# A mixed chunk of 42 hidden columns, earlier ones, later masks and fewer shift transfers in a fused two-block kernel

## The chip, the cores and the metric

The kernel runs on one core of a Trainium2 chip. A core has five engines with an instruction stream each: TensorE (PE, its weight loads PEld), VectorE (DVE), ScalarE (ACT), GpSimd (POOL) and SyncE (SP), and 16 DMA engines. The metric is the device time of one execution in microseconds.

## The reference, cut to what matters

The input is 8 sequences of 512 tokens with 256 channels, float32. The model is two gated residual steps. Step 0 adds (multi-head retention of the normalised input) times silu(local-attention network of the same). Step 1 adds (latent causal attention with 16 heads) times silu(mixture of 8 experts, the best two for each token). The local-attention network has two layers; the change touches its second half:

```python
x = x + o @ wo                                    # 8 heads of 64, window 128
h = shift_token(x)                                # second 128 channels: row of the token before
h = (h - mean) / sqrt(var + 1e-05) * lg + lb
a, g = split(h @ w1 + b1, 2)                      # w1: 256 x 1364, so 682 columns each
x = x + (a * gelu(g, approximate=False)) @ w2 + b2
```

## The kernel before, in words

Each engine's program is written out by hand in the order in which it is to run, and semaphores join them; nothing is scheduled by a planner. A sequence is an item: 512 tokens as 4 tiles (NT) of 128. The two layers of the local network make 16 items, numbered through. Stage k (0 to 15) ends item k (output projection, shift, normalisation, up and down projection) and beside it prepares item k+1 (QKV, rotary, heads' norms, scores). Stages 0 to 7 do layer 0 and the retention of the same item ("ret"). Stages 8 to 15 do layer 1 and latent attention and routing ("lat", "behind": the part for the item before; this part is absent in stage 8). Stage 15 ("last") prepares nothing. Then come 71 tiles of 128 routed tokens through the experts, and a final sum.

PSUM is two rings of four banks. Ring A (pA) is emptied by ScalarE, ring D (pD) by VectorE; `ring_a_jobs` and `ring_d_jobs` list the jobs in the order of TensorE's program, and a job waits until the job four banks earlier is emptied.

The parts that the change touches:

- Up projection, `up_projection` (through `project`, L722) in six chunks c of 120 hidden columns, 82 in the last. For each chunk TensorE makes the gate product into ring A and the value product into ring D, each as four instructions over 512 tokens. ScalarE's `gelu` (L1281) reads the gate and waits for the product of chunk c-2, whose buffer it takes. VectorE's `gate_up` (L1717) multiplies value and gelu into `hT`. Ahead of chunk 5 it sets rows from 64 on to one (L1714), and one of them carries the bias b2 through `down_projection`, which takes all six chunks.
- Between the chunks, TensorE does work of the prepared item (turns of heads, L761) and of latent attention (`latent_values` L888, `ranks` L915). VectorE does, behind chunk 0, the sums of squares of tile 3 (L1661), the scalings of tiles 2 and 3 (`scale_qk`, L1665) and the router's choice; behind these come chunks 1 to 5.
- Shifted rows: SP's program starts each stage with eight transfers inside SBUF, two for each tile: 127 rows moved down by one (L566), and the row of the tile before or zeros (L568, L570). VectorE's `shifted_stats` (L1631) waits for each tile by its own semaphore.
- Chain for the prepared item: VectorE's `rotary_parts` (L1655, L1657) and `square_sums`, GpSimd's `rotary_sum` (L1497) and `head_norms` (the roots, L1501), VectorE's `scale_qk`, TensorE's turns.
- Latent attention: VectorE's `clipped` (L1775) takes the scores of a pair of heads from ring D, ScalarE's exponential (L1307) follows, and GpSimd's `causal` (L1513, L1514, L1516) masks in place. The order of GpSimd in the tile loop of a stage is: masks of pair 4+t for t = 0, 1, 2, then the sum and the roots of tile t; behind the loop the masks of pair 7.
- Zeroed rows behind each expert's tokens: SP issues one fixed transfer (L624) and four whose address is read from the counts (L627), and four more inside `fetch(0)`, behind the first expert's first weights (L643) and ahead of the first fetch of tokens (L650), which waits for all of them and for GpSimd's scattered rows (L1527).

## Time and profile before

| quantity | value |
|---|---|
| median of 3 runs | 2845.77 us (2840.29 to 2845.85) |
| profiled execution | 2849.19 us, its span 2847.4 us |
| mean granted TensorE clock | 0.978 |
| VectorE busy | 1546.2 us (54%) |
| ScalarE busy | 1235.8 us (43%) |
| GpSimd busy | 1051.0 us (37%) |
| chain that ended last | PE 65%, issue 13%, DVE 10%, POOL 6%, ACT 3%, DMA 2% |

Busy time is summed over the span, so it mixes stages with different limits. The chain that ended last is followed back from the last instruction, each step to what released it. "Issue" is time for which the profile shows no wait. In the timelines each row is one instruction, or several alike run together, and the bracket behind it says how long the engine had been idle before it and who released it. SPq and ACTq are DMA issues.

### The profile page before, as it was taken

The page shows a single profiled execution, that of the slowest core. Times are in us where ns is not written, and L with a number is a line of the kernel's source. Part 1 is how long each engine was busy: PE and PEld are TensorE (multiplying, and loading weights), DVE is VectorE, ACT ScalarE, POOL GpSimd, SP SyncE. Part 2 cuts the span into 40 slices and gives each one's busy share as a digit, 9 for nine tenths or more (in the row PEclk, how much of TensorE's full clock was granted, in tenths as well). Part 3 has the DMA queues.
Part 4 walks back from the last instruction along what each step waited for, and adds up shares of the span by engine and source line. Part 5 has one row for each costly group of instructions (what it writes and reads, how often), then busy time and mean ns, then how long its engine had stood idle before and what let it go on. Part 6 is the DMA issues. An engine that isn't in the chain of part 4 may idle for free.

```text
span 2847.4 us, 41985 instructions
## 1 busy us (share of the span) xinstructions
PE 2703.8 (95%) x15582; PEld 1833.3 (64%) x15582; DVE 1546.2 (54%) x3730; ACT 1235.8 (43%) x2287; POOL 1051.0 (37%) x726
## 2 busy tenths in 40 slices
PE   6999999999999999999999999999997799999993
PEld 4575757566575757555555555555564578999993
DVE  6565566575666555677676767576855322100004
ACT  4454444545453444545454545454543234222222
POOL 5434243443434243445454536363623122111110
PEclk9999999999999999999999999999998899999997
DMA  4000000000001001101010101010000666899987
GB/s 143 12 16 26 26 16 30 27 27 16 26 16 57 18 24 52 61 5 53 4 53 5 53 4 45 12 39 19 30 34 23 235 247 250 304 365 365 360 334 243
DMA packets 85907, 261.83 MB, mean 92 GB/s; under 512 B 10668, under 2 KB 49916, under 8 KB 67020
## 3 DMA queue, kind: packets, MB, share of 16 engines
q1 hardware_dynamic: 75004, 237.19, 23.0%
q0 software_dynamic: 6480, 17.77, 1.7%
q10 hardware_dynamic: 4224, 4.19, 0.4%
q8 instruction: 128, 2.10, 0.3%
q14 instruction: 71, 0.58, 0.1%
HBM read 210.81 MB, written 44.11 MB: 90 GB/s over the span
## 4 chain that ended last, share of the span: by engine, by line
PE 65%; issue 13%; DVE 10%; POOL 6%; ACT 3%; DMA 2%; SPq 0%; POOLq 0%; DVEq 0%; ACTq 0%
PE s_pD L722 19%; PE s_pA L722 18%; PE s_pD L878 5%; PE s_pA L772 3%; PE s_pD L794 3%; PE s_pA L781 3%; PE s_pA L1167 2%; PE s_pD L1182 2%; POOL acc_s L1598 2%; DVE s_qk L1676 2%; POOL s_rinv L1501 2%; PE s_pA L761 1%; DMA s_z<-s_cur 1%; PE s_pA L733 1%; PE s_pA L888 1%
## 5 line engine op out<-in xcount | busy, mean ns | idle before, releaser
L1507 POOL TENSOR_TENSOR s_qk<-s_qk,s_rrec 128x1024 f32<-128x1024 f32 (+1 forms) x128 | 220.7, 1725 | 502.7 <-DVE s_rrec L1682 502.5
L722 PE MATMUL s_pA<-s_w_wqkv,s_curT 128*128 128x512 f32 x768 | 354.6, 602 | 5.6 <-ACT s_curT L1212 3.7
L1236 ACT ACTIVATE s_qk<-s_qk,s_mx 128x256 f32<-128x256 f32 (+1 forms) x512 | 239.8, 471 | 95.3 <-DVE s_mx L1676 95.3
L1775 DVE TENSOR_SCALAR s_pairs<-s_pD 128x1024 f32<-128x1024 f32 (+1 forms) x192 | 195.0, 1040 | 151.4 <-PE s_pD L878 150.1
L722 PEld LDWEIGHTS s_pA<-s_w_wqkv,s_curT 128*128 128x128 f32 x768 | 142.6, 191 | 176.7 <-issue 163.2
L1501 POOL TENSOR_TENSOR s_rinv<-s_ssq,s_half 128x16 f32<-128x16 f32 x64 | 230.1, 3596 | 59.5 <-DVE s_ssq L1661 59.5
L1598 POOL DMA_INDIRECT acc_s<-s_w_w,s_sq x71 | 68.5, 964 | 470.7 <-ACT s_w_w L1444 463.5
L2139 DVE COPY s_w_wo<-s_pD 128x256 f32<-128x256 f32 x71 | 29.9, 421 | 338.5 <-PE s_pD L1153 338.5
L1466 POOL TENSOR_TENSOR s_rs<-s_ve,s_half 128x4 f32<-128x4 f32 x40 | 42.0, 1050 | 433.4 <-DVE s_ve L1636 433.3
L878 PE MATMUL s_pD<-s_mixer 32*128 32x512 f32 (+3 forms) x1024 | 180.7, 467 | 11.9 <-DVE s_pairs L1775 9.0
L722 PE MATMUL s_pA<-s_zT,s_w_w 128*120 128x512 f32 (+1 forms) x384 | 183.8, 601 | 4.2 <-ACT s_pairs L1281 3.1
L1676 DVE CUSTOM_DVE_ANT_0 s_qk<-s_pA,s_maskw 128x256 f32<-128x256 f32 (+1 forms) x512 | 167.9, 386 | 25.3 <-PE s_pA L772 24.8
L722 PE MATMUL s_pD<-s_zT,s_w_w 128*120 128x512 f32 (+1 forms) x384 | 180.7, 593 | 0.0
L1497 POOL TENSOR_TENSOR s_qk<-s_qk,s_rot 128x1024 f32<-128x1024 f32 x64 | 151.1, 2361 | 51.8 <-DVE s_qk L1657 51.8
L1307 ACT ACTIVATE s_pairs<-s_pairs 128x2560 f32<-128x2560 f32 x64 | 149.7, 2339 | 44.2 <-DVE s_pairs L1775 44.0
L1218 ACT COPY s_qk<-s_pA 128x1024 f32<-128x1024 f32 x64 | 64.8, 1012 | 231.6 <-PE s_pA L722 231.6
L878 PEld LDWEIGHTS s_pD<-s_mixer 32*128 32x128 f32 x1024 | 89.3, 188 | 100.3 <-issue 50.6
L772 PE MATMUL s_pA<-s_qkT 64*128 64x256 f32 (+1 forms) x1024 | 134.2, 380 | 5.7 <-DVE s_mx L1676 3.8
L781 PE MATMUL s_pA<-s_ident,s_qk 128*128 128x128 f32 x896 | 126.9, 282 | 11.4 <-POOL s_qk L1507 6.5
L1665 DVE SCALAR_TENSOR_TENSOR s_qk<-s_rinv,s_qk 128x1024 f32<-128x1024 f32 x64 | 110.9, 1733 | 42.0 <-POOL s_rinv L1501 42.0
L722 PEld LDWEIGHTS s_pD<-s_zT,s_w_w 128*120 128x120 f32 (+1 forms) x384 | 68.6, 179 | 97.1 <-issue 93.1
L1444 ACT ACTIVATE s_w_w<-s_pD,s_w_w 128x256 f32<-128x256 f32 x71 | 33.6, 473 | 219.2 <-PE s_pD L1182 219.2
(268 smaller groups left out, 5724.6 us busy)
## 6 DMA issues: line engine op xcount, KB each, us to landing
s_qkT<-in_m_w SPq DMA_DIRECT2D x48, 1024.0 KB, 6.7
s_v_tm<-in_m_w SPq DMA_DIRECT2D x24, 1024.0 KB, 7.4
s_rot<-in_m_w SPq DMA_DIRECT2D x24, 1024.0 KB, 6.3
s_w_wqkv<-in_m_w SPq DMA_DIRECT2D x23, 1024.0 KB, 7.7
s_qk<-in_m_w SPq DMA_DIRECT2D x23, 1024.0 KB, 5.7
s_w_w<-rows_s SPq DMA_DIRECT2D x71, 129.0 KB, 6.0
s_cur<-in_x SPq DMA_DIRECT2D x8, 512.0 KB, 3.5
xn_s<-s_cur SPq DMA_DIRECT2D x8, 512.0 KB, 2.6
```

Source lines behind the costliest of these rows:

```text
L722: last = nc.tensor.matmul(out, lhs(c), rhs(c), start=(c == 0), stop=(c == n - 1))
L772: last = nc.tensor.matmul(ps[:, place(i) * 256 + lo * P:(place(i) + 1) * 256], qkT[r, h // 2, tile_cols(t)], qkT[r, 4 + h // 2, (t - 1 + l ...
L781: last = nc.tensor.transpose(ps[:, (2 * i + k) * P:(2 * i + k + 1) * P], prob[w % 3][:, i * 256 + k * P:i * 256 + (k + 1) * P], ident[:])
L878: last = nc.tensor.matmul(ps[:, 512 * i + col:512 * i + col + T - kt * P], KT[rows, g % 2, tile_cols(kt)], QT[rows, g % 2, kt * P:T], star ...
L1236: last = nc.scalar.activation(pi, pi, ACT.Exp, scale=-1.0, bias=mx[:, u, i:i + 1], accum_out=rsum[:, u, i:i + 1])
L1307: nc.scalar.activation(ph, ph, ACT.Exp, scale=1.0 / SQ24).then_inc(lexp, 1)
L1497: nc.gpsimd.tensor_tensor(qk[:, t, :], qk[:, t, :], rot[:, t % 2, :], ALU.add)
L1501: nc.gpsimd.tensor_tensor(rinv[:, t, :], ssq[:, t, :], half[:], ALU.pow).then_inc(rinv_rdy, 1)
L1507: nc.gpsimd.tensor_tensor(pi, pi, rrec[:, u, :].unsqueeze(2).broadcast_to((P, 4, 256 - lo)), ALU.mult).then_inc(p_rdy, 1)
L1598: nc.gpsimd.indirect_dma_start(out=S["acc"], out_offset=bass.IndirectOffsetOnAxis(ap=goal[:, w % NX:w % NX + 1], axis=0), in_=m_y[:, w % N ...
L1676: last = nc.vector.tensor_tensor_reduce(out=prob[u % 3][:, h], in0=ps[:, h], in1=maskw[:, lo:256], scale=-1.0, scalar=3e38, op0=ALU.add, o ...
L1775: nc.vector.tensor_scalar(Pl[:, w % SLOTS, :, ROUND_AT[r]:ROUND_AT[r] + ROUND_N[r]], ps[:, :, 0:ROUND_N[r]], 80.0, -80.0, ALU.min, ALU.max ...
```

## The change

- Chunks are now 42, 128, 128, 128, 128, 128 hidden columns. Chunk 0 has one product into ring D: 42 value columns, 22 columns of zeros, 42 gate columns (106 in all, `GATE` = 64). The job ("g", k, 0) leaves ring A. `gelu` of chunk 0 waits for this product and reads its rows 64 to 105; it increments `first_gelu`, for which `gate_up` of chunk 0 waits.
- The ones are set ahead of chunk 0 instead of chunk 5, before the wait for the product, in rows 32 to 63 of its buffer; row 42 carries b2.
- Shifted rows: five transfers instead of eight, two semaphores instead of four. Tiles 0 and 1 move in one transfer of 127 rows by two tiles, with two small ones; tiles 2 and 3 in one, with one small one of two rows.
- Except in the last stage, the masks of the seventh pair (index 6) stand ahead of tile 3's sum, that is behind tile 2's roots and not ahead of tile 2's sum.
- The zeroed rows of experts 4 to 7 are issued by ScalarE in stage 15, behind `values_in`, and not by SP in `fetch(0)`.

```diff
-HCH = 120
+HCH = 128
-HSZ = [min(HCH, HID - HCH * c) for c in range(NHC)]
+HSZ = [HID - HCH * (NHC - 1)] + [HCH] * (NHC - 1)
+HAT = [0] + [HSZ[0] + HCH * c for c in range(NHC - 1)]
+GATE = 64
+ONES = 32
+UPW = GATE + HSZ[0] + 2 * HCH * (NHC - 1)
...
-            if s.here:
+            if s.here and c:
                 j += [("g", k, c)]
...
-                    for t in range(NT):
-                        sp.wait_ge(outD, doneD["wo", k, t // 2])
-                        sp.dma_start(hB[1:P, t, :], cur[k % 2][0:P - 1, t, P:D]).then_inc(shifted[t], 16)
-                        if t == 0:
-                            sp.dma_start(hB[0:1, 0, :], I["zrow"]).then_inc(shifted[t], 16)
+                    for i in range(2):
+                        two = slice(2 * i, 2 * i + 2)
+                        sp.wait_ge(outD, doneD["wo", k, i])
+                        sp.dma_start(hB[1:P, two, :], cur[k % 2][0:P - 1, two, P:D]).then_inc(shifted[i], 16)
+                        if i == 0:
+                            sp.dma_start(hB[0:1, 0, :], I["zrow"]).then_inc(shifted[i], 16)
+                            sp.dma_start(hB[0:1, 1, :], cur[k % 2][P - 1:P, 0, P:D]).then_inc(shifted[i], 16)
                         else:
-                            sp.dma_start(hB[0:1, t, :], cur[k % 2][P - 1:P, t - 1, P:D]).then_inc(shifted[t], 16)
+                            sp.dma_start(hB[0:1, two, :], cur[k % 2][P - 1:P, 1:3, P:D]).then_inc(shifted[i], 16)
...
-            for e in range(E // 2):
-                zero_rows(e)
...
-                    for z in range(E // 2, E):
-                        zero_rows(z)
...
-                n = HSZ[c]
+                n = HCH if c else GATE + HSZ[0]
+                at = GATE + HSZ[0] + 2 * HCH * (c - 1) if c else 0
-                ps = slotA("g", b, c)
-                project(ps[0:n, 0:T], lambda k: W["w1"][:, k, HID + c * HCH:HID + c * HCH + n], lambda k: zT[:, k, :], DC).then_inc(mmA, 1)
+                if c:
+                    ps = slotA("g", b, c)
+                    project(ps, lambda k: W["w1"][:, k, at + HCH:at + 2 * HCH], lambda k: zT[:, k, :], DC).then_inc(mmA, 1)
                 ps = slotD("a", b, c)
-                project(ps[0:n, 0:T], lambda k: W["w1"][:, k, c * HCH:c * HCH + n], lambda k: zT[:, k, :], DC).then_inc(mmD, 1)
+                project(ps[0:n, 0:T], lambda k: W["w1"][:, k, at:at + n], lambda k: zT[:, k, :], DC).then_inc(mmD, 1)
...
-                ps = takeA("g", b, c)
+                at = 0 if c else GATE
+                if c:
+                    ps = takeA("g", b, c)
+                else:
+                    act.wait_ge(mmD, DJ["a", b, 0] + 1)
+                    ps = pD[:, colsD[DJ["a", b, 0]]]
                 if b > 0 or c >= 2:
                     act.wait_ge(outD, doneD["a", b, c - 2] if c >= 2 else doneD["a", b - 1, NHC - 1])
-                nc.scalar.activation(gl_of(b)[c % 2][0:n], ps[0:n, 0:T], ACT.Gelu, bias=W["b1"][0:n, 1, c:c + 1]).then_inc(outA, 1)
+                last = nc.scalar.activation(gl_of(b)[c % 2][0:n], ps[at:at + n, 0:T], ACT.Gelu, bias=W["b1"][at:at + n, 1, c:c + 1])
+                last.then_inc(outA if c else first_gelu, 1)
...
+                    if s.last and u == 5:
+                        act.wait_ge(zero_rdy, 2)
+                        act.wait_ge(weight_rdy, TOPK * LAST + 1)
+                        for e in range(E // 2, E):
+                            n = act.value_load(counts_i[0:1, e:e + 1], min_val=0, max_val=B * T)
+                            act.dma_start(S["rows"][bass.ds(n + e * REG, P), :], zrows).then_inc(zero_in, 16)
...
-                    if s.behind and t < (2 if s.last else 3):
+                    if s.behind and t < 2:
                         causal(b - 1, 4 + t)
+                    if s.behind and not s.last and t == 3:
+                        causal(b - 1, 6)
...
-                if c == NHC - 1:
-                    step(nc.vector.memset(hT_of(b)[NHC - 1][64:HCH], 1.0))
+                if c == 0:
+                    step(nc.vector.memset(hT_of(b)[0][ONES:2 * ONES], 1.0))
                 ps = take("a", b, c)
-                dve.wait_ge(outA, doneA["g", b, c])
+                if c:
+                    dve.wait_ge(outA, doneA["g", b, c])
+                else:
+                    dve.wait_ge(first_gelu, b + 1)
```

## Rows read from the trace of the kernel before

**Rows 1.** The page's first part: busy time and share, by engine.
```profile
PE 2703.8 (95%) x15582; PEld 1833.3 (64%) x15582; DVE 1546.2 (54%) x3730; ACT 1235.8 (43%) x2287; POOL 1051.0 (37%) x726
```

**Rows 2.** Windows: stretch, length, busy (x) PE PEld DVE ACT POOL, clock, DMA, GB/s.
```profile
82.00:1113.60 1031.60, 1023.14 (x5478) 657.34 (x5477) 629.23 (x1558) 482.70 (x1011) 401.44 (x213) 1.00 0.08 27
...
1240.40:2113.00 872.60, 844.78 (x4891) 504.42 (x4890) 615.30 (x1399) 450.74 (x775) 431.77 (x300) 0.99 0.08 27
...
2500.00:2780.00 280.00, 280.00 (x1934) 264.04 (x1933) 24.47 (x114) 64.05 (x116) 37.41 (x39) 1.00 0.95 355
```

**Rows 3.** Timeline, up-projection of stage 3: start, us, instruction, [idle before it, releaser].
```profile
521.20 1.88 PE L722 MATMUL s_pA<-s_zT,s_w_w 128*120 128x512 f32 x4
...
522.43 1.28 ACT L1281 ACT_TABLE_LOAD   x1
...
522.92 1.88 PE L722 MATMUL s_pD<-s_zT,s_w_w 128*120 128x512 f32 x4
...
523.72 0.69 ACT L1281 ACTIVATE s_pairs<-s_pA,s_w_b 120x512 f32<-120x512 f32 x1
...
524.83 0.75 DVE L1717 SCALAR_TENSOR_TENSOR s_pairs<-s_pD,s_w_b,s_pairs 120x512 f32<-120x512 f32 x1 [9.08 <-PE s_pD L722]
```

**Rows 4.** Timeline, end of the chain in stage 10.
```profile
1447.21 1.74 DVE L1665 SCALAR_TENSOR_TENSOR s_qk<-s_rinv,s_qk 128x1024 f32<-128x1024 f32 x1 [2.80 <-POOL s_rinv L1501]
...
1454.42 0.69 ACT L1281 ACTIVATE s_pairs<-s_pA,s_w_b 120x512 f32<-120x512 f32 x1 [5.86 <-DVE s_pairs L1717]
...
1455.16 1.98 PE L722 MATMUL s_pA<-s_zT,s_w_w 128*120 128x512 f32 x4 [0.51 <-ACT s_pairs L1281]
```

**Rows 5.** Groups by line and shape: a full-width weight over 256 columns.
```profile
L722 PE MATMUL s_pD<-s_w_wo,s_sq 128*128 128x256 f32 x512 | 113.2, 379 | 0.0
```

**Rows 6.** Timeline, chunk 5's ones in stage 3.
```profile
544.17 0.48 DVE L1714 MEMSET s_pairs<- 56x512 f32 x1 [0.16 <-issue]
```

**Rows 7.** Timeline, shifted rows and their statistics in stage 10.
```profile
1391.46 0.65 SPq L566 DMA_DIRECT2D s_z<-s_cur  x1
...
1393.81 2.40 SPq L570 DMA_DIRECT2D s_z<-s_cur  x1
...
1406.07 0.29 DVE L1631 BATCH_NORM_STATS2 s_stat<-s_cur 128x6 f32<-128x128 f32 x1 [2.29 <-DMA s_z<-s_cur]
```

**Rows 8.** Windows, while those transfers run.
```profile
1393.00:1398.00 5.00, 5.00 (x46) 2.24 (x46) 1.98 (x3) 0.43 (x1) 0.00 (x0) 1.00 0.07 21
```

**Rows 9.** Timeline, tile 1's scaling and turn in stage 8.
```profile
1149.93 2.64 DVE L1665 SCALAR_TENSOR_TENSOR s_qk<-s_rinv,s_qk 128x1024 f32<-128x1024 f32 x1
...
1153.65 1.04 PE L761 MATMUL s_pA<-s_ident,s_qk 128*128 128x128 f32 x8
```

**Rows 10.** Timeline, VectorE and GpSimd in stage 10.
```profile
1428.15 1.30 DVE L1655 TENSOR_TENSOR s_rot<-s_qk,s_w_fS 128x512 f32<-128x512 f32 x2
...
1431.73 0.73 POOL L1513 TENSOR_TENSOR s_pairs<-s_pairs,s_tri 128x256 f32<-128x256 f32 x1 [0.73 <-ACT s_pairs L1307]
...
1435.32 2.36 POOL L1497 TENSOR_TENSOR s_qk<-s_qk,s_rot 128x1024 f32<-128x1024 f32 x1
...
1435.73 3.12 DVE L1655 TENSOR_TENSOR s_rot<-s_qk,s_w_fS 128x512 f32<-128x512 f32 x2
...
1443.28 3.89 POOL L1501 TENSOR_TENSOR s_rinv<-s_ssq,s_half 128x16 f32<-128x16 f32 x1
```

**Rows 11.** Timeline, stage 15 and the step to the expert tiles.
```profile
2150.33 3.77 PE L722 MATMUL s_pA<-s_zT,s_w_w 128*120 128x512 f32 x4 [1.11 <-ACT s_zT L1254]
...
2223.25 4.29 SPq L627 DMA_DIRECT2D rows_s<-s_w_fC  x4
...
2235.06 0.66 PE L1153 MATMUL s_pD<-s_ident,s_w_w 128*128 128x128 f32 x2 [7.85 <-DMA s_w_w<-rows_s]
```

**Rows 12.** Timeline, scores of stage 8.
```profile
1195.76 2.08 PE L772 MATMUL s_pA<-s_qkT 64*128 64x256 f32 x8 [3.15 <-DVE s_mx L1676]
```

**Rows 13.** Windows, from the same moment.
```profile
1195.10:1201.90 6.80, 6.14 (x30) 4.96 (x32) 2.63 (x16) 5.41 (x15) 5.50 (x4) 0.50 0.00 0
```

More of the change, by code:

```diff
@@ L295, in stream_layers @@
         W = {}
-        by_layer = (("wqkv", [P, DC, 3 * INNER]), ("wo", [P, 4, D]), ("ln", [P, 2, DC]), ("w1", [P, DC, 2 * HID]),
+        by_layer = (("wqkv", [P, DC, 3 * INNER]), ("wo", [P, 4, D]), ("ln", [P, 2, DC]), ("w1", [P, DC, UPW]),
                     ("b1", [HCH, 2, NHC]), ("w2", [HCH, NHC, D]), ("qks", [P, 2, 2, DH]))
@@ L471, in stream_layers @@
         xs_in = sem("xs_in")
-        shifted = [sem(f"shifted{t}") for t in range(NT)]
+        shifted = [sem(f"shifted{i}") for i in range(2)]
         x1_kept = sem("x1_kept")
@@ L495, in stream_layers @@
         shift_rdy = sem("shift_rdy")
+        first_gelu = sem("first_gelu")
         fin_silu = sem("fin_silu")
@@ L624, in _ @@
             sp.dma_start(S["rows"][E * REG:E * REG + P, :], zrows).then_inc(zero_in, 16)
-            def zero_rows(e):
+            for e in range(E // 2):
                 n = sp.value_load(counts_i[0:1, e:e + 1], min_val=0, max_val=B * T)
                 sp.dma_start(S["rows"][bass.ds(n + e * REG, P), :], zrows).then_inc(zero_in, 16)
-            for e in range(E // 2):
-                zero_rows(e)
             sp.wait_ge(table, 1)
@@ L808, in up_projection @@
             def up_projection(b, c):
-                n = HSZ[c]
                 if c == 0:
                     pe.wait_ge(outA, doneA["zT", b, 1])
-                ps = slotA("g", b, c)
-                project(ps[0:n, 0:T], lambda k: W["w1"][:, k, HID + c * HCH:HID + c * HCH + n], lambda k: zT[:, k, :], DC).then_inc(mmA, 1)
+                n = HCH if c else GATE + HSZ[0]
[3 more added lines that the diff above has]
+                    project(ps, lambda k: W["w1"][:, k, at + HCH:at + 2 * HCH], lambda k: zT[:, k, :], DC).then_inc(mmA, 1)
                 ps = slotD("a", b, c)
-                project(ps[0:n, 0:T], lambda k: W["w1"][:, k, c * HCH:c * HCH + n], lambda k: zT[:, k, :], DC).then_inc(mmD, 1)
+                project(ps[0:n, 0:T], lambda k: W["w1"][:, k, at:at + n], lambda k: zT[:, k, :], DC).then_inc(mmD, 1)
             def down_projection(b, i):
-                rows = [min(HCH, HSZ[c] + (c == NHC - 1)) for c in range(NHC)]
+                rows = [HSZ[c] + (c == 0) for c in range(NHC)]
                 if i == 0:
@@ L1700, in shifted_stats @@
                 for t in tiles:
-                    dve.wait_ge(shifted[t], 32 * (b + 1))
+                    dve.wait_ge(shifted[t // 2], (32 if t // 2 else 48) * (b + 1))
                     ln_stats(t, halves(b, t))
@@ L2217, in arrange @@
     r["w_ln"] = np.stack([np.stack([per(g), per(b)], 1) for g, b in zip(a["L0_ffn_ln_g"], a["L0_ffn_ln_b"])], 1)
-    r["w_w1"] = np.stack([ch(w) for w in a["L0_ffn_w1"]], 1)
+    up = []
+    for c in range(NHC):
+        value = a["L0_ffn_w1"][:, :, HAT[c]:HAT[c] + HSZ[c]]
+        gate = a["L0_ffn_w1"][:, :, HID + HAT[c]:HID + HAT[c] + HSZ[c]]
+        room = np.zeros(value.shape[:2] + (0 if c else GATE - HSZ[0],), np.float32)
+        up += [value, room, gate]
+    r["w_w1"] = np.stack([ch(w) for w in np.concatenate(up, 2)], 1)
     b1 = np.zeros((HCH, DEPTH, 2, NHC), np.float32)
@@ L2224, in arrange @@
             for i in range(2):
-                b1[0:n, l, i, c] = a["L0_ffn_b1"][l, i * HID + c * HCH:i * HID + c * HCH + n]
-            w2[0:n, l, c] = a["L0_ffn_w2"][l, c * HCH:c * HCH + n]
-        w2[HSZ[-1], l, NHC - 1] = a["L0_ffn_b2"][l]
+                at = 0 if c or not i else GATE
+                b1[at:at + n, l, i, c] = a["L0_ffn_b1"][l, i * HID + HAT[c]:i * HID + HAT[c] + n]
+            w2[0:n, l, c] = a["L0_ffn_w2"][l, HAT[c]:HAT[c] + n]
+        w2[HSZ[0], l, 0] = a["L0_ffn_b2"][l]
     r["w_b1"], r["w_w2"] = b1, w2
```

## The prediction

> **What bounds the kernel now.** I read the page's first part: TensorE is busy 95% of the span [rows 1]. The table by stretch says where that is a bound [rows 2]: 1023 of 1032 us from 82 to 1113.6 (stages 0 to 7, layer 0 with retention), 280 of 280 in the expert tiles, but 845 of 873 in stages 9 to 14 (layer 1 with latent attention). So I went through one stage of each kind by the timeline. In a retention stage TensorE goes through the up-projection without a gap: one projection starts 1.72 us after the one before (521.20, 522.92), and VectorE has idled 9.08 us before its first product [rows 3]. In a latent stage TensorE arrives at the gate product of chunk 4 and waits 0.51 us for ScalarE's gelu of chunk 3; that gelu had waited 5.86 us for VectorE, which stood behind the router block, which stood behind the scaling of tile 3, which had waited 2.80 us for GpSimd's roots of tile 3 [rows 4]. A latent stage is set by a VectorE/GpSimd chain, and TensorE runs just ahead of it. Saving TensorE work there buys nothing unless the chain shortens too.
>
> **Mixed chunk, stages 0 to 7.** The 682 hidden columns need six chunks before and after, but value and gate of the 42-column chunk now share one product of 106 columns: 11 projections of 12 remain. A projection is four hardware matmuls over 512 columns, 1.72 us by the start times above; the weight's columns (120 before, 128 or 106 after) don't enter the length of the moving side, so I take it unchanged. The down projection keeps six chunks and its count of matmuls; a 128-row weight over 256 columns is in the trace with a mean of 379 ns [rows 5], so zero. Gelu and the VectorE product run along 512 elements whatever the partitions: zero. The first gelu now follows the joint product and reads partitions 64 to 105 of the other PSUM tensor, which no row shows; nearest is the gelu of [rows 3], 0.69 us, bounds 0.6 to 1.4. It stands behind a table load of 1.28 us that starts at 522.43 [rows 3], not behind TensorE (the joint product ends at 522.9), so VectorE's first product stays at 524.8 and costs nothing. TensorE runs 1.72 us further ahead, and no wait of a retention stage is close enough to take that back. 8 stages x 1.72 = **13.8 us**.
>
> **Ones ahead of the wait.** A memset of 0.48 us, with 0.16 before it [rows 6], goes from chunk 5 to chunk 0. In stages 0 to 7 VectorE idles there (the 9.08 us): nothing. In latent stages VectorE has no pause there and the reduction for tile 3's roots stands behind it: 0 to 0.64 us a stage; I come to it below.
>
> **Shifted rows in five transfers.** Before: four transfers of 127 rows of 512 B, each with a small one. SP needs 0.65 us for the first of tile 0 and 2.40 for the small one of tile 1 [rows 7]; eight issues are some 11 us, five some 7. But issue is not what VectorE waits for. While the transfers run the DMA engines are busy 0.07, which is one of 16, at 21 GB/s [rows 8]. At that rate 127 x 512 B take 3.1 us, all four 12.4 us from about 1392.6 (just behind the first issue) to 1405.0, and tile 3's statistics start at 1406.07 after 2.29 us of waiting for them [rows 7]. A pair of tiles is 254 rows. If it too goes to one engine, the last byte lands as before, but tile 2's statistics, which were done in the gap, now come behind it together with tile 3's: the pair ends 0.45 to 0.75 us later; I take 0.45. If it is spread over two or more, it ends up to 3 us earlier. I take one engine, as the row has it. The Trainium skill, DMA: Bandwidth & Descriptors, "Why a DMA increments its semaphore by 16 and not by 1", says that the engine count is the largest one up to 16 that divides the slowest dimension, and gives 127 partitions one engine; by it the pair gets one too. No row shows a pair. In stages 0 to 7 the delay disappears in the 9.08 us.
>
> **Stage 8.** VectorE runs without a pause from the statistics to the scaling of tile 1, which ends at 1152.57 (1149.93 + 2.64); TensorE takes that tile's second turn at 1153.65 now and would be there at 1151.93 [rows 9]. With 0.75 us of delay the tile is ready at 1153.3: **0.3 us** stay of 1.72.
>
> **Stages 9 to 14, the masks of the seventh pair.** Before, GpSimd idled 0.73 us, did the masks (1431.73 to 1435.32), summed tile 2 (2.36), took its roots, summed tile 3 and took its roots, 1443.28 to 1447.17. VectorE and GpSimd don't overlap freely: the two rotary products take 1.30 us alone and 3.12 beside the sum [rows 10]. So I lay the new order out as taking turns. Sum of tile 2 at 1431.0 (the idle time is gone) to 1433.4; VectorE's scaling of tile 1, which stood beside the masks, waits for it to 1434.6; clipping (about 2.3) to 1436.9; roots of tile 2 to 1437.0; then the masks (0.7, 0.7, 1.3 alone) and the rotary work (0.65, 0.65, 1.23) alternate to 1441.9; sum to 1444.25; roots to 1448.15. That is 1.0 us later than 1447.17: the idle time won is less than the collision of masks and rotary that is bought. If the masks ran free beside the rotary work, the roots would come about 1.2 earlier instead. The Trainium skill, SBUF — State Buffer, "Who interferes with whom", has a VectorE operation with two SBUF inputs and a GpSimd operation that reads SBUF exclude each other for a whole instruction; by it the three masks meet the products one by one, as in the sequence above, and the 3.12 agrees. Now the memset makes VectorE's reduction the later input of the roots (0.35), and the transfers add 0.45: **+1.8 us per stage, x6 = +10.8**. Bounds: -1.2 and +3.5 (rival 3). TensorE's 1.72 turn into waiting.
>
> **Stage 15.** No tile is prepared ahead. The first gate product takes four matmuls at the lower clock, 3.77 us [rows 11]; the joint product takes its place, chunk 1 follows 1.8 to 2 us sooner: **1.8 us**.
>
> **Zeroed rows for experts 4 to 7, issued by ScalarE.** Before, SP issued them behind the first expert's weights (2223.25, 4.29 us), and TensorE idled 7.85 us to 2235.06 for the first rows of tokens [rows 11]. After, ScalarE issues them from about 2216.7 on; I take the same 4.29 for it. Queued behind them are the two copies that turn the attention of item 6, now until about 2222.0, against 2221.7 at which VectorE released TensorE: 0.3 us at most, hidden in the 7.85. The fetch then waits for the scattered rows, whose last bytes go out about 2 us before those of the zeros; with the issue time: **2.4 us**, bounds 1 and 5.3. The expert tiles are full on TensorE [rows 2], so this reaches the end.
>
> **The sum.** 13.8 + 0.3 + 1.8 + 2.4 - 10.8 = 7.5 us off the profiled execution's 2849.2 (span 2847.4), so 2841.7. That execution is 3.4 above the median of 2845.8; the same 7.5 off the median: **2838 us**. What a measurement of this kernel can tell from no change is 0.2%, 5.7 us.
>
> **Rivals.**
> 1. The latent chain stays where it is (the turns of masks and rotary fall better, the memset is absorbed): 18.3 us off, 2827.5. For it: the idle 0.73 us is real. Against: the 3.12 us row. 20%.
> 2. The pair of tiles goes to two or more DMA engines: statistics end up to 3 us earlier, and the chain shortens by the 1.2 above; stage 8 keeps its 1.72. 6 x 1.2 + 1.4 more than rival 1 gives: 2819. Against: the 0.07. 12%.
> 3. Slower: TensorE idles about 3 us in one piece before the latent values of group 3 in each latent stage (it comes 1.3 us sooner, and the masks of pair 7, which follow tile 3's roots, end 1.8 later). After 3.15 us of idling at 1195.76 [rows 12] the granted clock was 0.50 for 6.8 us [rows 13], the 1.2 GHz level. A drop behind each of the six costs up to 1.7 us where 3.4 us of matmuls run at it. With a chain of +1.8 that makes +3.5 per stage: 18.3 - 21 = -2.7, so 2848.5. It turns to slower at 3.05 us per stage. For it: the idle piece is as long as that one. Against: the chain, not TensorE, is then the bound, and hides some of it. 18%.
> 4. My forecast: 45%. Others, such as a gelu that is slow from a shifted partition: 5%.
>
> **How the numbers follow.** The forecast's own range is 2833 to 2844, since the chain is worth +1.0 to +2.7 per stage. The range 2819 to 2850 takes in the rivals to their middles. Faster by over 0.2% (below 2840): rivals 1 and 2 and six tenths of mine, 0.61; within 0.2%: the rest of mine and most of rival 3, 0.31; slower 0.08.
>
> **What would show it.** The distance from one stage's first up-projection to the next one's 1.72 us shorter in retention stages. In a latent stage: statistics of tiles 2 and 3 back to back after one wait; roots of tile 3 later against the stage's start; TensorE waiting 2 to 3 us before latent values of group 3; SP issuing five transfers in 7 us. The wait before the first expert tile down from 7.85 to about 5.4. Wrong if latent stages shorten by over 1 us: then the turns or the one-engine reading fail.

## The result

The changed kernel takes 2851.56 us (median of 9 runs, 2850.36 to 2853.39), the kernel before 2845.03 (9 runs, 2840.29 to 2846.19). The ratio is 1.002 with an interval of 1.0012 to 1.0029: slower by 6.5 us, and the interval leaves 1 out. The profiled execution of the change took 2852.14 us (span 2850.4). That of before took 2849.19, some 4 us over its own median, so the two traces differ by only 3.0 us, and the stages below add up to that; the other 3.5 us of the difference of the medians belong to no stage that a trace shows.

I measure a stage from the first matmul of its output projection to that of the next, in the timeline (before, stage 10 begins at 1387.08 and stage 11 at 1530.87: 143.8). "Last" is stage 15 up to the first expert product. The kernels from "eight transfers" on are the experiments. Times in us. The stages are those of one profiled execution, whose own time stands in the column "profiled"; then come the median of the timed runs and the median of the kernel before, run on the same chip. The experiments ran on four chips, between which the kernel before differs by up to 3.8 us, so medians of different rows are compared by their distance from the last column.

| kernel | stages 0 to 7 | stage 8 | 9 to 14 | last | profiled | median | before, same chip |
|---|---|---|---|---|---|---|---|
| before | 1031.6 | 126.8 | 872.5 | 122.1 | 2849.2 | 2845.0 | |
| changed | 1028.9 | 128.4 | 880.4 | 118.1 | 2852.1 | 2851.6 | 2845.0 |
| predicted difference | -13.8 | -0.3 | +10.8 | -4.2 | | -7.5 | |
| measured difference | -2.7 | +1.6 | +7.9 | -4.0 | +3.0 | +6.5 | |
| eight transfers (e1) | 1027.4 | 126.6 | 874.8 | 119.6 | 2845.9 | 2844.2 | 2845.8 |
| 128 rows (e2) | 1019.5 | 127.9 | 888.9 | 118.2 | 2850.3 | 2844.7 | 2845.8 |
| old mask order (e3) | 1028.9 | 128.4 | 882.5 | 120.4 | 2856.1 | 2852.8 | 2845.8 |
| zeros on SP (e4) | 1029.0 | 128.5 | 882.3 | 121.8 | 2858.5 | 2854.5 | 2845.8 |
| spread transfers (e5) | 1029.0 | 126.1 | 862.7 | 117.7 | 2832.2 | 2831.0 | 2845.1 |
| 64 rows (e6) | 1029.0 | 128.4 | 881.1 | 117.5 | 2853.0 | 2853.0 (one run) | 2845.1 |
| eight, old masks (e7) | 1027.4 | 127.0 | 877.1 | 117.2 | 2844.3 | 2844.3 | 2845.1 |
| eight, no memset (e8) | 1027.4 | 127.2 | 870.2 | 117.8 | 2837.8 | 2844.3 | 2845.1 |
| three edits (e9) | 1019.5 | 125.1 | 865.7 | 116.9 | 2823.8 | 2822.1 | 2848.9 |
| three edits, old masks (e10) | 1019.5 | 123.8 | 866.5 | 117.7 | 2824.2 | 2818.6 | 2848.9 |
| before, spread (e11) | 1031.6 | 126.8 | 862.4 | 121.4 | 2839.1 | 2839.1 | 2848.9 |
| filled wait (e12) | 1027.4 | 128.4 | 880.9 | 118.2 | 2851.2 | 2851.5 | 2846.9 |

### The profile page after: what moved, and what is told of

Same layout as the page of the kernel before. It is cut to its first block, busy times and chain, and to the rows that moved or that the text cites. A ratio compares the mean times of both kernels' runs of the same rounds, so it can differ in the third digit from the quotient of the medians.

```text
span 2850.4 us, 41810 instructions
## 1 busy us (share of the span) xinstructions
PE 2702.0 (95%) x15518; PEld 1818.9 (64%) x15518; DVE 1532.7 (54%) x3730; ACT 1237.1 (43%) x2287; POOL 1056.3 (37%) x726
## 4 chain that ended last, share of the span: by engine, by line
PE 63%; issue 14%; DVE 11%; POOL 5%; DMA 4%; ACT 2%; SPq 2%; POOLq 0%; DVEq 0%; ACTq 0%
PE s_pD L724 18%; PE s_pA L724 17%; PE s_pD L882 5%; PE s_pA L774 3%; PE s_pA L783 3%; PE s_pD L796 3%; PE s_pA L1171 2%; PE s_pD L1186 2%; DMA s_z<-s_cur 2%; POOL acc_s L1616 2%; POOL rows_s L1543 1%; PE s_pA L735 1%; PE s_pA L892 1%; PE s_pA L763 1%; DVE s_qk L1694 1%
## 5 line engine op out<-in xcount | busy, mean ns | idle before, releaser
L724 PE MATMUL s_pA<-s_w_wqkv,s_curT 128*128 128x512 f32 x768 | 364.8, 617 | 5.6 <-ACT s_curT L1216 3.7
L724 PE MATMUL s_pD<-s_zT,s_w_w 128*128 128x512 f32 (+1 forms) x384 | 183.0, 599 | 1.1 <-ACT s_zT L1258 1.1
L1513 POOL TENSOR_TENSOR s_qk<-s_qk,s_rot 128x1024 f32<-128x1024 f32 x64 | 151.0, 2359 | 55.1 <-DVE s_qk L1675 55.1
L724 PE MATMUL s_pA<-s_zT,s_w_w 128*128 128x512 f32 x320 | 152.1, 598 | 3.1 <-ACT s_pairs L1290 3.1
L724 PE MATMUL s_pD<-s_w_w,s_pairs 43*128 43x256 f32 x480 | 137.7, 402 | 0.0
L783 PE MATMUL s_pA<-s_ident,s_qk 128*128 128x128 f32 x896 | 126.8, 282 | 3.6 <-POOL s_qk L1523 3.2
```

Source lines behind the costliest of these rows:

```text
L724: last = nc.tensor.matmul(out, lhs(c), rhs(c), start=(c == 0), stop=(c == n - 1))
L783: last = nc.tensor.transpose(ps[:, (2 * i + k) * P:(2 * i + k + 1) * P], prob[w % 3][:, i * 256 + k * P:i * 256 + (k + 1) * P], ident[:])
L1513: nc.gpsimd.tensor_tensor(qk[:, t, :], qk[:, t, :], rot[:, t % 2, :], ALU.add)
```

## The profile after

First the busy times from the page of the profile, answering [rows 1], then the windows that answer to [rows 2] and [rows 8], with one more at 1410.4.

```profile
PE 2702.0 (95%) x15518; PEld 1818.9 (64%) x15518; DVE 1532.7 (54%) x3730; ACT 1237.1 (43%) x2287; POOL 1056.3 (37%) x726
```

```profile
82.30:1111.20 1028.90, 1020.36 (x5446) 651.70 (x5445) 631.23 (x1558) 483.07 (x1011) 401.74 (x213) 1.00 0.08 27
...
1239.70:2120.00 880.30, 845.61 (x4866) 497.02 (x4865) 600.40 (x1398) 451.44 (x775) 436.37 (x300) 0.99 0.08 27
...
1393.00:1398.00 5.00, 5.00 (x45) 2.26 (x45) 1.98 (x3) 0.55 (x1) 0.00 (x0) 1.00 0.07 19
...
1410.40:1413.80 3.40, 3.40 (x5) 1.35 (x4) 3.37 (x4) 0.87 (x1) 2.45 (x3) 0.50 0.00 0
```

TensorE's share is 95% as before; it says nothing. The windows do: in stages 9 to 14 TensorE is still busy for 845.6 us, but in 880 us, not in 873. While the shift transfers run the DMA share is 0.07 as before, at 19 GB/s: a pair of tiles goes to one engine. And at 1410.4, 23.5 us into stage 10, the granted clock is 0.50 for 3.4 us; below, such a stretch is called a drop of the clock. The other five of the stages 9 to 14 have one there too, 24 us in.

The up-projection of stage 3, answering [rows 3]: joint product of 106 columns, table load, gelu of its rows 64 to 105, next product, VectorE.

```profile
519.90 1.88 PE L724 MATMUL s_pD<-s_zT,s_w_w 128*106 128x512 f32 x4
...
521.13 1.28 ACT L1290 ACT_TABLE_LOAD   x1
...
522.43 0.68 ACT L1290 ACTIVATE s_pairs<-s_pD,s_w_b 42x512 f32<-42x512 f32 x1
...
522.49 1.88 PE L724 MATMUL s_pA<-s_zT,s_w_w 128*128 128x512 f32 x4
...
523.25 0.74 DVE L1738 SCALAR_TENSOR_TENSOR s_pairs<-s_pD,s_w_b,s_pairs 42x512 f32<-42x512 f32 x1 [6.75 <-ACT s_pairs L1290]
```

This part went as forecast. The next product starts 2.59 us after the joint one, with a turn of heads between them (before, the value product and that turn stood there); gelu from a shifted partition takes 0.68 us; VectorE waits for ScalarE and TensorE never for either.

The loss in the same stage stands at its end, in the down projection. Groups by shape in a stretch of 129 us around stage 2 (337 to 466), first before, then after:

```profile
L722 PE MATMUL s_pD<-s_w_w,s_pairs 120*128 120x256 f32 x24 | 5.9, 383 | 0.0
...
L722 PE MATMUL s_pD<-s_w_w,s_PT_even 120*128 120x256 f32 x16 | 4.1, 379 | 0.0
...
L722 PE MATMUL s_pD<-s_w_w,s_pairs 83*128 83x256 f32 x8 | 2.4, 379 | 0.0
```

```profile
L724 PE MATMUL s_pD<-s_w_w,s_pairs 128*128 128x256 f32 x24 | 6.9, 396 | 0.0
...
L724 PE MATMUL s_pD<-s_w_w,s_PT_even 128*128 128x256 f32 x16 | 4.1, 379 | 0.0
...
L724 PE MATMUL s_pD<-s_w_w,s_pairs 43*128 43x256 f32 x8 | 2.7, 418 | 0.0
```

The count is 48 in both, but the sum is 12.4 us before and 13.7 after. The eight products over 43 rows take 418 ns and not 379, and of their neighbours over 128 rows some take longer too (mean 396). By their start times, products follow each other in 0.216 us, but in 0.31 to 0.32 us in the two or three steps around each change between 43 and 128 rows, some 12 steps in a stage; with 120 and 83 rows no change has such a step. That is the 1.2 us by which a retention stage missed its 1.72: it went from 129.27 to 128.75, 0.52 less. Why the array does this is not shown.

Stage 10, shifted rows and statistics, answering [rows 7]:

```profile
1391.34 0.72 SPq L572 DMA_DIRECT2D s_z<-s_cur  x1
...
1392.10 4.68 SPq L574 DMA_DIRECT2D s_z<-in_zrow  x1
...
1397.44 0.71 SPq L572 DMA_DIRECT2D s_z<-s_cur  x1
...
1406.60 0.29 DVE L1649 BATCH_NORM_STATS2 s_stat<-s_cur 128x6 f32<-128x128 f32 x1 [4.28 <-DMA s_z<-s_cur]
...
1407.36 0.29 DVE L1649 BATCH_NORM_STATS2 s_stat<-s_cur 128x6 f32<-128x128 f32 x1
...
1408.96 1.14 PE L882 MATMUL s_pD<-s_mixer 32*128 32x384 f32 x8 [2.41 <-DVE s_pairs L1796]
```

Before, only tile 3 was still to do when the wait ended at 1406.07. Now the wait ends at 1406.60 (stage 10 starts 0.12 earlier, so 0.65 late), tile 2 comes first, and tile 3 begins 0.76 behind it: 1.41 us late in all. VectorE's clipping of scores stands behind, TensorE waits 2.41 us for it instead of 1.00, and the clock drops.

Where the 0.65 comes from: the single packets of the trace, 509 before and 511 after, follow each other without a gap of 0.3 us in both kernels, so the rows are never held up by SP's 4.68 us of issuing. They start 0.11 us later against the stage's start and lose some 0.5 more in the first 2 us, before the second pair is issued; from then on the lag stays between 0.6 and 0.8. The same stretch before, then after:

```profile
1392.70:1394.70 2.00, 2.00 (x11) 1.25 (x9) 0.51 (x1) 0.00 (x0) 0.00 (x0) 1.00 0.07 19
```

```profile
1392.70:1394.70 2.00, 2.00 (x11) 1.13 (x9) 0.63 (x1) 0.00 (x0) 0.00 (x0) 1.00 0.06 13
```

Why a pair of tiles starts more slowly than a single tile is not shown.

The same stage's end of chain, answering [rows 10]: rotary products, two of the three masks, the memset, the sum of tile 3, its roots.

```profile
1438.40 1.82 DVE L1673 TENSOR_TENSOR s_rot<-s_qk,s_w_fS 128x512 f32<-128x512 f32 x2
...
1438.65 1.02 POOL L1529 TENSOR_TENSOR s_pairs<-s_pairs,s_tri 128x256 f32<-128x256 f32 x1
...
1440.77 2.24 POOL L1532 TENSOR_TENSOR s_pairs<-s_pairs,s_tri 128x512 f32<-128x512 f32 x1
...
1442.05 0.48 DVE L1732 MEMSET s_pairs<- 32x512 f32 x1 [0.16 <-issue]
...
1442.98 2.35 POOL L1513 TENSOR_TENSOR s_qk<-s_qk,s_rot 128x1024 f32<-128x1024 f32 x1
...
1445.74 3.82 POOL L1517 TENSOR_TENSOR s_rinv<-s_ssq,s_half 128x16 f32<-128x16 f32 x1 [0.41 <-DVE s_ssq L1679]
```

Roots of tile 3 start 58.8 us into the stage, 56.2 before, and they now wait for VectorE's sum of squares (0.41 us), not for GpSimd's own sum.

The step to the expert tiles, answering [rows 11]:

```profile
2221.34 4.19 SPq L634 DMA_DIRECT2D rows_s<-s_w_fC  x4
...
2223.70 3.83 ACTq L1431 DMA_DIRECT2D rows_s<-s_w_fC  x4
...
2238.10 0.66 PE L1157 MATMUL s_pD<-s_ident,s_w_w 128*128 128x128 f32 x2 [3.99 <-DMA s_w_w<-rows_s]
```

TensorE waits 3.99 us instead of 7.85. That is nearly the whole gain of the last stage: TensorE begins this wait 114.1 us into the stage, and 114.2 before.

## The experiments

**e1: the eight transfers back.**

```diff
-sp.dma_start(hB[1:P, two, :], cur[k % 2][0:P - 1, two, P:D]).then_inc(shifted[i], 16)
+sp.dma_start(hB[1:P, t, :], cur[k % 2][0:P - 1, t, P:D]).then_inc(shifted[t], 16)
...
-dve.wait_ge(shifted[t // 2], (32 if t // 2 else 48) * (b + 1))
+dve.wait_ge(shifted[t], 32 * (b + 1))
```

> The changed kernel with the eight shift transfers and four semaphores of before; all else stays. Theory S (the pair transfers make the latent stages late): tile 3's statistics stand 1.3 us earlier in each of the stages 9 to 14, TensorE's wait before the scores of the pair there falls from 2.4 to about 1.0 us, the granted clock no longer drops 24 us into these stages, and a stage goes from 146.5 to about 144 us: about 2 to 2.5 us for each of six, 1 for stage 8, so 2836 to 2840 against 2851.6. Theory C (the chain over masks, memset and roots of tile 3 sets these stages, as predicted): only the transfers' share goes, 0.5 us a stage, so about 2848. Retention stages unchanged at 128.75 by both.

2844.16 us (2839.8 to 2848.53, 10 runs), ratio to before 0.9997 (0.9987 to 1.0007): 7.4 us under the changed kernel (8.1 by the distances from before). In stage 10 (starts at 1381.39), tile 3's statistics, the scores behind them, and tile 3's sum and roots:

```profile
1400.53 0.29 DVE L1647 BATCH_NORM_STATS2 s_stat<-s_cur 128x6 f32<-128x128 f32 x1 [2.37 <-DMA s_z<-s_cur]
...
1402.12 1.14 PE L880 MATMUL s_pD<-s_mixer 32*128 32x384 f32 x8 [1.15 <-DVE s_pairs L1794]
...
1435.65 2.35 POOL L1511 TENSOR_TENSOR s_qk<-s_qk,s_rot 128x1024 f32<-128x1024 f32 x1
...
1438.41 3.82 POOL L1515 TENSOR_TENSOR s_rinv<-s_ssq,s_half 128x16 f32<-128x16 f32 x1 [0.41 <-DVE s_ssq L1677]
```

Tile 3's statistics stand 19.1 us into the stage (19.6 and 20.4 for the two tiles with pairs), TensorE's wait is 1.15 instead of 2.41, and no stage but one has a drop near 24 us. The roots start at 57.0, 1.8 earlier than with pairs, and the stage is 144.6 against 146.4. The signs of theory S came, but not its full size: the time is 2844 and not 2836 to 2840. Stages 9 to 14 are 874.8 and not the 868 or so expected: 0.8 of the 2.6 us at the roots is of other origin (e7, e8), and three stages have drops elsewhere.

**e2: 128 rows of chunk 0 in the down projection.**

```diff
-rows = [HSZ[c] + (c == 0) for c in range(NHC)]
+rows = [HCH] * NHC
...
+nc.vector.memset(hT_of(b)[0][GATE:HCH], 1.0)
```

> The changed kernel with the down projection reading all 128 rows of chunk 0: rows above b2's are set to one and meet weights of zero, so the result is the same; one more memset for each item. Theory W (a product over 43 rows between products over 128 rows costs a gap of 0.1 us at each change, 12 of them in a stage): the gaps go, a retention stage goes from 128.75 to about 127.5, latent stages lose up to 1.2 where TensorE sets them, so 2836 to 2842 against 2851.6. Rival (the gaps come from other work between, such as waits for VectorE's chunk or the order of the chunks): nothing changes but the memset, 2851 to 2853.

2844.70 us (2840.69 to 2851.74, 10 runs), ratio 0.9997. Groups of the same stretch:

```profile
L724 PE MATMUL s_pD<-s_w_w,s_pairs 128*128 128x256 f32 x32 | 8.0, 383 | 0.0
...
L724 PE MATMUL s_pD<-s_w_w,s_PT_even 128*128 128x256 f32 x16 | 4.1, 379 | 0.0
```

12.1 us for the same 48 products. A retention stage is 127.55, so the full 1.72 less than 129.27, and stages 0 to 7 are 9.4 us shorter than with 43 rows. The rival is out. Part of it was lost again: by the medians the edit gains 6.9 us (7.6 by the distances from before). In the profiled execution, which lies 5.6 over the median, stages 9 to 14 grew by 8.5 us. Some 3.7 of these, 0.6 a stage, stand at the roots of tile 3, which now wait 1.04 us for VectorE and not 0.41: the second memset stands ahead of their sum. The rest goes with eight drops of the clock (one of 6.8 us; three of them late, at 119 and 146 us) where there had been six. That the one more memset or the earlier TensorE brings these drops was not told apart.

**e6: 64 rows.**

```diff
-rows = [HSZ[c] + (c == 0) for c in range(NHC)]
+rows = [HCH if c else GATE for c in range(NHC)]
```

> The changed kernel with 64 rows of chunk 0 in the down projection instead of 43; the rows of one above b2's meet weights of zero. Tells what in the 43 rows costs: if it is that they are no more than half of the array's 128 (before, 83 rows cost nothing), a retention stage stays at 128.75 us and the mean of these products near 418 ns; if it is the odd count, it falls to 127.6 us, as with 128 rows.

One run, 2852.98 us. Groups of the same stretch:

```profile
L724 PE MATMUL s_pD<-s_w_w,s_pairs 128*128 128x256 f32 x24 | 6.9, 396 | 0.0
...
L724 PE MATMUL s_pD<-s_w_w,s_PT_even 128*128 128x256 f32 x16 | 4.1, 379 | 0.0
...
L724 PE MATMUL s_pD<-s_w_w,s_pairs 64*128 64x256 f32 x8 | 2.7, 418 | 0.0
```

64 rows cost what 43 do, to the nanosecond, and the stage stays at 128.75. Before, 83 rows cost nothing. So it is the small number of rows beside products over more, not the odd count; where between 64 and 83 rows the cost begins was not measured.

**e3: the masks of the seventh pair back ahead of tile 2's sum.**

```diff
-if s.behind and t < 2:
+if s.behind and t < (2 if s.last else 3):
     causal(b - 1, 4 + t)
-if s.behind and not s.last and t == 3:
-    causal(b - 1, 6)
```

> The changed kernel with the seventh pair's masks back ahead of tile 2's sum. Theory C (as predicted, the masks collide with the rotary products and make tile 3's roots 1.0 us late in stages 9 to 14): 1.0 us a stage back, so about 2845.6. Theory S (the shift transfers and the clock drop at 24 us set these stages): the stages stay within 0.5 us, 2849 to 2854; it may even be slower, as the idle time of GpSimd comes back.

2852.77 us (2850.42 to 2856.82, 6 runs), ratio 1.0026 (1.0013 to 1.0039). Stage 10 starts at 1386.90; sum of tile 3 and its roots:

```profile
1442.90 2.35 POOL L1513 TENSOR_TENSOR s_qk<-s_qk,s_rot 128x1024 f32<-128x1024 f32 x1
...
1445.89 3.82 POOL L1517 TENSOR_TENSOR s_rinv<-s_ssq,s_half 128x16 f32<-128x16 f32 x1 [0.65 <-DVE s_ssq L1677]
```

The roots start at 59.0 with the old order, 58.8 with the new, in all six stages. Theory C is out: the new order does not cost 1.0 us a stage.

**e4: the zeroed rows of experts 4 to 7 back on SP.** The loop with its four issues goes from ScalarE's stage 15 to `fetch(0)`.

> The changed kernel with the zeroed rows of experts 4 to 7 issued by SP behind the first expert's weights, as before. The prediction's step has 2.4 us for them, so 2854; bounds 1 to 5.3. A rival, that the scattered rows and not the zeros end the wait now: under 1 us, 2852. The distance from the last stage's start to the first expert product goes from 118.1 to 120.5 by the first, and stays by the second.

2854.47 us (2853.73 to 2858.5, 5 runs), ratio 1.0035 (1.0021 to 1.0049), 2.9 more than the changed kernel. SP's issues and the first expert product:

```profile
2233.44 4.28 SPq L651 DMA_DIRECT2D rows_s<-s_w_fC  x4
...
2244.02 0.66 PE L1160 MATMUL s_pD<-s_ident,s_w_w 128*128 128x128 f32 x2 [8.33 <-DMA s_w_w<-rows_s]
```

The wait is 8.33 instead of 3.99 us; the distance of "last" is 121.8 against 118.1. The step is worth 2.9 by these medians (2.2 by the distances from before on each chip) and 3.7 by the traces; its rival, under 1 us, is out by the wait.

**e5: 112 and 15 rows instead of 127.**

```diff
-sp.dma_start(hB[1:P, two, :], cur[k % 2][0:P - 1, two, P:D]).then_inc(shifted[i], 16)
+sp.dma_start(hB[1:113, two, :], cur[k % 2][0:112, two, P:D]).then_inc(shifted[i], 16)
+sp.dma_start(hB[113:P, two, :], cur[k % 2][112:P - 1, two, P:D]).then_inc(shifted[i], 16)
```

> The changed kernel with each transfer of 127 rows by two tiles split into one of 112 rows and one of 15; seven transfers instead of five. Theory S (one DMA engine at 21 GB/s is what makes the statistics late, so spreading is the cure): the DMA share while they run rises well over 0.07, tile 3's statistics follow tile 1's without a wait of over 1 us, the drop of the clock 24 us into a latent stage goes, stages 9 to 14 take 875 us or less against 880.4, stage 8 one to two less than 128.4; total 2838 to 2843. Rival (the issue by SP or the small one-row transfers set the time): statistics of tile 3 stay at 19 to 20 us into the stage, and nothing changes.

2831.03 us (2828.58 to 2836.71, 4 runs), ratio 0.9956 (0.9939 to 0.9972). Windows, then SP's first and last issue and the statistics of tiles 2 and 3 in stage 10:

```profile
1388.50:1390.50 2.00, 2.00 (x11) 1.77 (x10) 0.00 (x0) 0.00 (x0) 0.00 (x0) 1.00 0.22 58
...
1392.00:1394.00 2.00, 2.00 (x31) 0.85 (x32) 1.29 (x2) 0.00 (x0) 0.00 (x0) 1.00 0.23 60
```

```profile
1388.23 0.64 SPq L572 DMA_DIRECT2D s_z<-s_cur  x1
...
1393.33 0.69 SPq L578 DMA_DIRECT2D s_z<-s_cur  x1
...
1399.24 0.29 DVE L1650 BATCH_NORM_STATS2 s_stat<-s_cur 128x6 f32<-128x128 f32 x1
...
1400.01 0.29 DVE L1650 BATCH_NORM_STATS2 s_stat<-s_cur 128x6 f32<-128x128 f32 x1
```

The DMA share is 0.22, 58 GB/s, where it was 0.07, and VectorE waits for no tile: its four tiles follow each other. Tile 3's statistics stand 16.2 us into the stage, 4.2 earlier than with pairs of 127 rows. Five of six stages have no drop and take 143.2 to 143.5. The rival is out. That is 20.5 us less than the changed kernel (20.0 by the two traces) and 13.1 less than the eight transfers of e1.

**e7 and e8: memset and masks by the roots.** e7 is e1 with e3's edit. e8 is e1 with no memset: the one of b2 comes from the biases (zero weights, value bias 1/0.8413, gate bias 1), so the joint product has 107 columns.

> The changed kernel with the eight transfers and with the old place of the seventh pair's masks: what is left is the mixed chunk, the memset ahead of it and ScalarE's zeroed rows. In stage 10 tile 3's roots started 56.2 us into the stage before and 57.0 with the eight transfers alone. The predicted step (masks +1.0, memset +0.35) expects 56.0 here; the theory that the masks are neutral or a gain and the memset with the chunk ahead of the sum of squares costs 0.5 to 0.8 expects 57.0 to 57.3. Stages 9 to 14: 868 by the first, 875 to 877 by the second.

> The changed kernel with the eight transfers and no memset: the one that carries b2 comes out of the product itself (zero weights, biases that make value times gelu one), so the joint product has 107 columns and chunk 0 of VectorE 43 rows. If the memset is what makes tile 3's sum of squares the later input of the roots, they start 56.4 to 56.6 us into stage 10 against 57.0 with the memset, and the stage is 0.4 to 0.6 shorter than 144.6; if the masks are what delays them, 57.0 stays.

2844.34 us each (10 runs each). The roots of tile 3 in stage 10 of e8, which starts at 1382.11:

```profile
1438.71 3.90 POOL L1516 TENSOR_TENSOR s_rinv<-s_ssq,s_half 128x16 f32<-128x16 f32 x1
```

They start at 57.1 in e7, 57.0 in e1, 56.6 in e8 and 56.2 before. With the memset VectorE is late and the order of the masks moves nothing at the roots (57.1 against 57.0); the sum ahead of them starts 0.2 later with the new order (54.3 against 54.1). Without the memset GpSimd is late, and the new order has 56.6 where before had 56.2; but the statistics, too, come 0.2 later there (19.2 against 19.0), so only about half of this is the masks'. The medians of e1, e7 and e8 don't differ: what separates them per stage, 0.4 us, is less than what drops of the clock do (stages 9 to 14 of e8 have two, of e7 four, 870.2 and 877.1).

**e9, e10, e11: the version that beats both, and what the rest is worth.** e9 joins e5, e8's biases and the down projection over 128 rows of chunk 0, where the unused rows hold old finite values against weights of zero, with one memset at the start. e10 is e9 with e3's edit. e11 is the kernel before with e5's seven transfers.

> The changed kernel with three edits together: seven transfers of 112 and 15 rows, the down projection over all 128 rows of chunk 0 (its unused rows hold old finite values against weights of zero, so no memset is needed but one at the start), and the one for b2 from the biases. If the effects add: retention stages 127.6 us, 1.15 less than 128.75, stages 9 to 14 about 0.4 us shorter each than the 143.3 with the seven transfers alone, so 2831 - 9.2 - 2.4 = 2819, range 2814 to 2826. Rival: TensorE, coming earlier to its waits in the latent stages, idles long enough for the clock to drop there, as with the memset and 128 rows (888.9 against 880.4 for stages 9 to 14), which would leave 2825 to 2832.

> The kernel of the three edits together, with the seventh pair's masks back ahead of tile 2's sum. Without the memset the roots of tile 3 wait for GpSimd and not for VectorE, so here the order of the masks must show if it matters at all: the prediction's step has the new order 1.0 us a stage later, so this kernel 6 us faster than with the new order; if the new order is neutral, within 2 us; the shift of tile 3's sum by 0.2 us seen so far would make it 1 us faster.

> The kernel before with nothing changed but the transfers, seven of 112, 15 and single rows instead of eight. Before, VectorE waited 2.29 us for tile 3's rows in stage 10, so tile 3's statistics come 2.8 us earlier, TensorE's scores let 1.2 through, stages 9 to 14 fall from 145.4 to about 143.5 on the mean and stage 8 by 1: 2845 - 12 = 2833, range 2829 to 2838. If the drops of the clock at 115 us stay in four of six stages, 2838 to 2841. It tells what the rest of the change is worth beside these transfers.

e9: 2822.13 us (2816.0 to 2824.02, 4 runs), ratio 0.9902 (0.9886 to 0.9919). e10: 2818.61 us (2816.89 to 2824.23, 4 runs), 0.9895 (0.9878 to 0.9911). e11: 2839.11 us (2834.72 to 2839.79, 5 runs), 0.9964 (0.995 to 0.9978). Roots of tile 3 in stage 10 of e9 (starts at 1369.91) and of e10 (1368.78):

```profile
1425.05 3.89 POOL L1519 TENSOR_TENSOR s_rinv<-s_ssq,s_half 128x16 f32<-128x16 f32 x1
```

```profile
1423.78 3.89 POOL L1519 TENSOR_TENSOR s_rinv<-s_ssq,s_half 128x16 f32<-128x16 f32 x1
```

55.1 and 55.0 us: in the cleanest pair, too, the order of the masks is worth 0.1. The 3.5 us between the two medians are no more than the spread of four runs each, so the times do not decide it. That holds for stages without a drop: where one falls 30 us into a stage, as in stages 11 and 13 of e9, the roots start at 56.8. e9 lies 26.7 us under before on the same chip, e11 9.8: the mixed chunk with its rows mended, the biases and ScalarE's zeroed rows are worth some 17 us beside the transfers. The 2819 expected of e9 was 26 under 2845, so by the kernel before on its own chip it came as expected, and so did its retention stages (127.6); in its profiled execution, 1.7 over the median, stages 9 to 14 took 865.7 with five drops and not 860. e11 is 9.8 under where 12 were expected: of the four late drops one is left, but three stages have one at 30 us.

**e12: TensorE's wait filled.** In stages 9 to 14 four matmuls without use stand in the wait of 2.4 us.

```diff
+latent_scores(b - 1, 5, (0,))
+filler(k + 1)          # 4 matmuls over 512 columns into the next QKV bank
+latent_scores(b - 1, 5, (1,))
```

> The changed kernel with one more product without use in each of the stages 9 to 14: four matmuls over 512 tokens, 1.7 us, into the bank that the next QKV product overwrites, put where TensorE waits 2.4 us for VectorE's clipping behind the late statistics. It fills the idle time and moves nothing else. If the drop of the granted clock 24 us into these stages is a part of the cost of its own, beside the 1.4 us of lateness, it goes, and stages 9 to 14 fall from 880.4 by 1 to 1.7 each, so total 2851.6 - 8 = 2844 (2841 to 2847). If the drop is only a companion, because VectorE's chain sets these stages anyway, 879 to 881 stays, as 2851.

2851.48 us (2849.24 to 2853.27, 10 runs), ratio 1.0016 (1.0006 to 1.0025); that of the changed kernel is 1.0020 (1.0012 to 1.0029). The filler and the scores behind it, then tile 3's roots, in stage 10 (starts at 1384.71):

```profile
1404.22 1.98 PE L724 MATMUL s_pA<-s_curT,s_w_wqkv 128*128 128x512 f32 x4
...
1406.80 1.14 PE L882 MATMUL s_pD<-s_mixer 32*128 32x384 f32 x8 [0.59 <-DVE s_pairs L1809]
```

```profile
1443.08 3.82 POOL L1530 TENSOR_TENSOR s_rinv<-s_ssq,s_half 128x16 f32<-128x16 f32 x1 [0.39 <-DVE s_ssq L1692]
```

None of the six drops at 24 us is left, and stages 9 to 14 take 880.9 all the same. The roots start at 58.4 instead of 58.8 in each of them, so the drop was 0.4 us of the lateness and the transfers the other 1.4. The four stages without any drop take 146.4 on the mean, against 146.7 in the changed kernel; the two with a late drop, at 117 us, take 147.7 and use up what the others gain. So the drop at 24 us is little more than a companion, as VectorE's chain sets the stage. That a late drop costs more is read from stages with and without one; no experiment took it away.

## Why the prediction was wrong

It forecast 2838 in a range to 2850 and got 2851.6, on the other side of before. By its own steps:

- **Mixed chunk, stages 0 to 7: the step that failed.** It said of the down projection "keeps six chunks and its count of matmuls ... so zero". The upward half of the step was right: 1.72 us less (e2 shows all of it). But the row it read, 128 rows at 379 ns, says nothing of 42 and one rows. The eight products over 43 rows and their neighbours cost 1.2 us a stage, 9.4 us in stages 0 to 7. With this term the same sum would have been 2848. What is left to 2851.6 is a drop of the clock in stage 6 (132.0 us, and 130.5 in e1 without it), the 1.9 us of stage 8, and a share of the 3.5 us that no stage shows. The trace of before had a hint: products over 64 rows (L942) took 297 ns there, those over 128 rows with the same 128 columns (L733) 272. I checked the dimension that grew (120 to 128) and not the one that shrank (83 to 43).
- **Shifted rows: mechanism right, size wrong.** One engine at about 20 GB/s, tile 2's statistics behind the wait: so it was. The Trainium skill's rule (DMA: Bandwidth & Descriptors, "Why a DMA increments its semaphore by 16 and not by 1") gives 127 rows one engine, 112 rows 16 and 15 rows 15. The traces agree as far as they go: a share of 0.07 for the first, about one of 16, and 0.22 in e5, three to four busy on the mean; how many took part is not shown. But 0.45 was too little. The statistics of a tile are 0.76, and the last byte came 0.65 later, not "as before", since the first 2 us of the pair ran at 13 GB/s and not at 19. (The forecast had five issues in some 7 us; they took 11.7, from 1391.34 to 1403.00, but no row waited for them.) So 1.4 us, and 0.4 more by the drop of the clock: 1.8 a stage for stages 9 to 14, and stage 8 came out at +1.6 instead of -0.3. Without the pairs it is 126.6 (e1), only 0.2 under before: of the 1.72 that should have been left there without a delay hardly anything was. Why is not shown; both kernels have a drop of 6.8 us in stage 8.
- **Masks: predicted +1.0, measured 0.1 to 0.2** at the last sum (e1 against e7, e9 against e10), and nothing behind it where VectorE is late (e3). Taking turns was right as a picture: after, the masks run 4.3 us from 1438.65 to the sum (3.6 before) and the two rotary products 1.82. But the sequence came out shorter than I laid it: in e1 the last sum starts 54.3 us into the stage, 53.9 before, so 0.4 later and not 0.9, and about half of that is the later statistics. The terms that I listed add up to 1442.1 and not 1441.9, which makes the miss 0.2 larger. The Trainium skill's rule (SBUF — State Buffer, "Who interferes with whom") names who collides, and the trace agrees (1.82 us beside masks, 1.30 alone); the length of the schedule it doesn't give.
- **Memset: 0.35 predicted, 0.4 measured** (e1 against e8).
- The sum for stages 9 to 14, +10.8, came out as +7.9, and that it is this close is luck: too much for the masks, too little for the transfers, and the drops of the clock moved (four late ones before, six early ones after). The traced execution of before is the one with the four late drops, and lies 4 us over its median, so against the median these stages may have lost more than 7.9; no trace of such an execution is there to show it.
- **Stage 15 and the zeroed rows: 4.2 predicted, 4.0 measured, the sum right by luck.** The zeroed rows alone are worth 3.7 and not 2.4 by the traces (e4; 2.2 to 2.9 by the medians), and the wait in front of the expert tiles fell by 3.9. The joint product is worth 0.3 and not 1.8: e4, which has it, takes 121.8 where before took 122.1. The up-projection does end 1.7 us sooner (its last product starts 63.5 us into the stage, 65.2 before), but other waits follow, and TensorE reaches the end of the stage only 0.1 us sooner.
- **Rivals.** Rival 3 had the right sign and the wrong place: TensorE's wait before the latent values was 0.98 us, 66.2 us into the stage, and not 3; the drop came 24 us into the stage, behind the statistics, and e12 shows that there it costs 0.4 us and not 1.7. Rival 2, the spread transfer, did not happen by itself. It had the transfers 8.6 us better than before's eight; measured are 9.8 (e11 against before) and 13.1 (e5 against e1), so its price was, if anything, low.

What stays open: why e2 and e9 get late drops that e5 hardly has, why e9, e10 and e11 have drops at 30 us, and why stage 6 has a drop at 112 us in the changed kernel and in e5 but not in e1 or e12.

## What to carry to other kernels

The joint product did what was forecast of it in the retention stages; what was missed stood in another product over the same chunk. When a chunk is made uneven, read each product that uses it for every dimension that changes, the contraction rows too, and look for a row of that size. When transfers are merged, ask what had been done between their ends: the merged wait ends with the last byte, and all the work that used the gaps stands behind it. Here, splitting 127 rows into transfers of 112 and 15 was worth 9.8 us in the kernel before and 20.5 in the changed one, more than anything else tried on that path. And when kernels are timed on different chips, compare each with the same reference on its own chip.
